# An early flag, a reordered last tile, and products that nothing reads at both ends of a gated layer kernel

## What is computed

```python
x = x + tanh(g0) * matmul(fake_quant(layernorm(x)), fake_quant(ctx))
h = layernorm(x)                               # the same row, updated
logits = h @ Wr.T                              # 4 experts, the best 2 are kept
mid    = einsum('tf,erf->ter', h, A)           # 4 experts of rank 16
delta  = sum_e softmax(kept logits)[e] * (mid[e] @ B[e].T) * SCALE
x = x + tanh(g1) * delta
```

## Time and profile before

| | before |
|---|---|
| median of 3 runs (lowest, highest) | 384.49 us (383.94, 385.21) |
| the profiled execution's own time | 386.0 us |
| its span, first to last instruction | 384.3 us |
| mean granted clock of TensorE | 0.961 of 2.4 GHz |
| busy: PE, DVE, ACT, POOL | 331.1, 290.6, 251.1, 95.9 us |
| data moved by DMA | 69.17 MB |

### The profile page before, as it was taken

How to read it: one execution, slowest core, us unless ns; L and a number is a source line. 1 busy time by engine, 2 the same in 40 slices (tenths; PEclk the granted TensorE clock), 3 DMA queues, 4 the chain that set the end, 5 groups by cost and what they waited for, 6 DMA issues and landing times. The chain is left out here.

```text
span 384.3 us, 6347 instructions
## 1 busy us (share of the span) xinstructions
PE 331.1 (86%) x2325; PEld 187.1 (49%) x2325; DVE 290.6 (76%) x715; ACT 251.1 (65%) x206; POOL 95.9 (25%) x107
## 2 busy tenths in 40 slices
PE   0148989999996689999989999999999999999374
PEld 0013434445654555555556556565556565646152
DVE  3677698679997899989756786869595969674834
ACT  1756948959999899499798065655556474743230
POOL 3100140003554341051045050504141322323000
PEclk9998999999999699999999999999999999999865
DMA  7999999950036779873641432232323201111022
GB/s 223 417 417 419 422 417 422 417 190 0 3 108 235 283 269 348 257 256 93 184 161 57 165 127 93 113 107 110 111 107 113 95 18 66 45 56 56 0 109 110
DMA packets 19185, 69.17 MB, mean 180 GB/s; under 512 B 2256, under 2 KB 2256, under 8 KB 19024
## 3 DMA queue, kind: packets, MB, share of 16 engines
q1 hardware_dynamic: 19152, 68.73, 47.9%
HBM read 51.94 MB, written 16.78 MB: 179 GB/s over the span
## 5 line engine op out<-in xcount | busy, mean ns | idle before, releaser
L658 PE MATMUL ps_main<-q,q1T 128*128 128x512 f16 x832 | 197.5, 379 | 2.1 <-ACT q1T L459 1.5
L658 PEld LDWEIGHTS ps_main<-q,q1T 128*128 128x128 f16 x832 | 77.3, 98 | 87.2 <-issue 9.0
L445 ACT ACTIVATE c_code<-q,small_tile 128x1024 uint8<-128x1024 f32 x62 | 74.7, 1239 | 24.6 <-DVE q L1118 12.7
L469 ACT ACTIVATE h_parts<-xr,small_tile 128x2048 f16<-128x2048 f32 x16 | 33.5, 2094 | 45.1 <-DVE small_tile L1196 45.1
L389 POOL TENSOR_TENSOR h_parts<-work,h_parts 128x512 f16<-128x512 f32 x30 | 34.9, 1185 | 65.9 <-ACT work L475 65.9
L1118 DVE TENSOR_SCALAR q<-c_code,small_tile 128x1024 f16<-128x1024 f16 x64 | 36.1, 566 | 15.9 <-ACT c_code L445 15.6
L1179 DVE SCALAR_TENSOR_TENSOR xr<-ps_main,small_tile,xr 128x512 f32<-128x512 f32 x52 | 38.7, 745 | 8.3 <-PE ps_main L658 8.1
L1252 DVE TENSOR_TENSOR xr<-ps_delta,xr 128x512 f32<-128x512 f32 x62 | 41.2, 681 | 4.9 <-PE ps_delta L740 3.3
L1123 DVE BATCH_NORM_STATS2 small_tile<-xr 128x6 f32<-128x512 f32 x64 | 40.9, 682 | 5.0 <-DMA xr<-in_x 5.0
L1184 DVE BATCH_NORM_STATS2 small_tile<-xr 128x6 f32<-128x512 f32 x64 | 43.6, 688 | 0.9
L481 ACT COPY hT<-ps_turn 128x1024 f16<-128x1024 f16 x32 | 31.4, 1007 | 17.9 <-PE ps_turn L692 17.8
(11 more groups left out here) (119 smaller groups left out, 393.4 us busy)
## 6 DMA issues: line engine op xcount, KB each, us to landing
q<-in_ctx SPq DMA_DIRECT2D x62, 512.0 KB, 8.7
xr<-in_x SPq DMA_DIRECT2D x32, 512.0 KB, 5.2
out_x<-xr SPq DMA_DIRECT2D x30, 512.0 KB, 2.8
h_parts<-in_B SPq DMA_DIRECT2D x1, 1024.0 KB, 16.4
q1T<-in_ctx SPq DMA_DIRECT2D x2, 512.0 KB, 8.4
out_x<-xr SPq DMA_DIRECT2D x4, 256.0 KB, 2.3
xr<-in_A SPq DMA_DIRECT2D x1, 544.0 KB, 17.0
small_tile<-in_params SPq DMA_DIRECT2D x1, 3.0 KB, 2.6
```

The costliest lines, as they stand in the source:

```text
L445: nc.scalar.activation(c_byte[:, i % 2, :], stage(i), ACT.Identity, bias=par[:, 3:4], scale=inv_s[:, 1:2]).then_inc(row_scaled, 1)
L469: nc.scalar.activation(h_hi[:, :], xr[:, b % RING, :], ACT.Identity, bias=h_bias[:, b % 2:b % 2 + 1], scale=h_rstd[:, b % 2:b % 2 + 1]).th ...
L658: mm = pe.matmul(product_bank(b, n)[:, :], q1T_of(b)[:, k, :], q2[:, batch(b), k, cols(n)], start=(k == 0), stop=(k == KT - 1))
```

## The change

Five things change.

1. `rests_of_points`, with it the flag, moves ahead of the first statistics on DVE.
2. ACT quantizes tile 0 (`scale_x(0)`) between the first and the second half row rather than behind both.
3. A new helper `keep_busy(n)` issues `n` products of 128 x 512 into `ps_main[0]` that nothing reads. It is called with 3, 7, 7 and 8 around the first two tiles' turns, and with 12 and 10 in the last tile.
4. The last tile's `h_hi` is made in two halves with a semaphore of their own, and each half of `h_lo` waits only for its half. `turn_hi` of the last tile moves ahead of the deltas 2 and 3 of tile 14. Turns, deltas and mid products are interleaved.
5. `last_delta` finishes one bank before it begins the next.

The diff, cut to its core:

```diff
@@ ACT
             scale_row(0)
+            scale_x(0)
             scale_row(1)
-            scale_x(0)
...
-            high_part(LAST)
+
+            act.wait_ge(h_bias_ready, TILES)
+            act.wait_ge(hi_turned, 2 * LAST)
+            act.wait_ge(h_lo_ready, 4 * LAST)
+            for h in range(2):
+                nc.scalar.activation(h_hi[:, half(h)], xr[:, LAST % RING, half(h)], ACT.Identity,
+                                     bias=h_bias[:, LAST % 2:LAST % 2 + 1], scale=h_rstd[:, LAST % 2:LAST % 2 + 1]).then_inc(last_hi, 1)
@@ PE
+            def keep_busy(n):
+
+                for _ in range(n):
+                    pe.matmul(ps_main[0][:, :].rearrange("p (a m) -> p a m", m=P), ident_h[:, :],
+                              ident_h[:, :].unsqueeze(1).to_broadcast([P, NB, P]), start=True, stop=True)
...
             def turn_hi(b, h):
-                pe.wait_ge(h_hi_ready, b + 1)
+                if b == LAST:
+                    pe.wait_ge(last_hi, h + 1)
+                else:
+                    pe.wait_ge(h_hi_ready, b + 1)
...
                 banks = ps_delta + ps_main
-                for n in range(2):
+                for n in range(NB):
                     pe.matmul(banks[n][:, :], gT_hi[:, :], lora_bT[:, cols(n)], start=True, stop=False)
-                pe.wait_ge(gT_ready, TILES)
-                for n in range(2):
-                    pe.matmul(banks[n][:, :], gT_lo[:, :], lora_bT[:, cols(n)], start=False, stop=True).then_inc(delta_done, 1)
-                for n in range(2, NB):
-                    pe.matmul(banks[n][:, :], gT_hi[:, :], lora_bT[:, cols(n)], start=True, stop=False)
+                    pe.wait_ge(gT_ready, TILES)
                     pe.matmul(banks[n][:, :], gT_lo[:, :], lora_bT[:, cols(n)], start=False, stop=True).then_inc(delta_done, 1)
...
                 pe.wait_ge(ident_ready, 2)
+                keep_busy(3)
                 turn_q1(0, 0)
+                keep_busy(7)
                 rows(0, 0, 0, 5, general)
+                keep_busy(7)
                 turn_q1(1, 0)
+                keep_busy(8)
                 rows(1, 0, 0, 3, general)
...
-                for n in range(NB):
-                    delta(LAST - 1, n)
+                delta(LAST - 1, 0)
+                delta(LAST - 1, 1)
+                pe.wait_ge(x1_ready, NB * LAST + 3)
+                keep_busy(12)
                 turn_hi(LAST, 0)
                 turn_hi(LAST, 1)
+                delta(LAST - 1, 2)
                 mid_hi(LAST, 0)
+                turn_lo(LAST, 0)
+                delta(LAST - 1, 3)
                 mid_hi(LAST, 1)
-                turn_lo(LAST, 0)
                 turn_lo(LAST, 1)
                 mid_lo(LAST, 0)
                 mid_lo(LAST, 1)
+                keep_busy(10)
                 turn_gate(LAST, TILES)
                 last_delta()
@@ DVE
             parameters()
+            rests_of_points()
             stats_x(0, 0)
             stats_x(0, 1)
             var_x(0)
-            rests_of_points()
             scale_of_x(0)
...
             dve.wait_ge(h_lo_ready, 4 * LAST)
+            dve.wait_ge(lo_turned, 2 * LAST)
             for h in range(2):
                 nc.vector.tensor_scalar(work[h], ...).then_inc(h2_ready, 1)
-            dve.wait_ge(h2_ready, 2 * TILES)
-            dve.wait_ge(lo_turned, 2 * LAST)
-            dve.wait_ge(h_hi_ready, TILES)
             for h in range(2):
+                dve.wait_ge(h2_ready, 2 * LAST + h + 1)
+                dve.wait_ge(last_hi, h + 1)
                 nc.vector.tensor_tensor(h_lo[:, half(h)], work[h], h_hi[:, half(h)], ALU.subtract).then_inc(h_lo_ready, 2)
```

More of the change, by code:

```diff
@@ L193, in build @@
         lo_turned, loT_ready = sem("lo_turned"), [sem("loT_ready0"), sem("loT_ready1")]
+        last_hi = sem("last_hi")
         hi_used, lo_used, mids_read, mids_scaled = sem("hi_used"), sem("lo_used"), sem("mids_read"), sem("mids_scaled")
```

## The result

| | before | after |
|---|---|---|
| median (lowest, highest), 4 runs each, taken in turn | 384.46 us (383.94, 385.21) | 375.45 us (374.84, 376.49) |
| ratio with its 95% interval | | 0.9767 [0.9739, 0.9795] |
| the profiled execution's own time, its span | 386.0, 384.3 us | 376.5, 374.7 us |
| mean granted clock | 0.961 | 0.982 |

The changed kernel is 9.0 us faster; 9.7 were forecast. The profiled execution of it was the slowest of the four, and its span of 374.7 is 0.7 to 1.6 above the others (374.0, 373.3, 373.1).

What follows compares the result with a forecast made beforehand. PE was taken as the bound in the middle, with time to be had only where PE waits at both ends. Start 3.0 plus last tile 6.8 made 9.8 us off 386.0; the median forecast was 374.8, range 372.0 to 379.0.

Steps and rivals of the forecast that it cites:

- the two terms: Start and last tile: 3.0 us from the earlier start plus 6.8 us from the last tile, together 9.8 us.
- the first term: Start: an earlier first product brings the scales of `A` 3.0 us earlier, carried to the end; bounds 0 and 3.8.
- The first product: PE at the start: code follows the earlier flag, first product at about 12.3, tile 0's turn done at 14.6 instead of 18.9.
- I take this as one delay that follows the flag: Start: the 6.56 us from flag to first transpose (flag load, branch, code behind it) move with the flag.
- DVE's code row: Around `A`: the half row's code beside POOL's first pass, 2.51 us, can't gain more than the scales do.
- From there on I find no wait with a fixed time: Middle, behind `A`: streams are relative to each other, so 3.0 us at 46 us stay 3.0 us at 350.
- The last tile: Last tile: mid products 5.8 us earlier, gate's turn 0.15 shorter, `last_delta` 0.85 less, together 6.8 us.
- The flag that gives nothing: Rival at the start: code arrives at 17.9 whatever the flag does, or low-clock products eat 1.5 us; 377.0, chance 0.17.
- the clock that falls: Rival in the last tile: clock falls, mid products gain about 2.5 us, ten products stick out by 1.7; 380.7, chance 0.11.
- The slower rival: Rival at the start: code at 17.9 and 25 exposed products cost up to 10.7 us; 388.4, chance 0.04.

Runs made afterwards that it cites:

- the flag moved back: Changed kernel with the flag's instructions put back behind tile 0's statistics on DVE, all added products kept: 377.52 us, ratio 0.9827 to the kernel before.
- the start's part alone: Kernel before plus only the early flag, ACT's swap and the 25 products around the first two turns: 381.58 us against 384.49, ratio 0.9931.
- the kernel without products: Changed kernel with all six `keep_busy` calls (47 products) left out, all orders as changed: 377.82 us, ratio 0.9826 to the kernel before.
- the end's part: Changed kernel with flag, ACT's swap and the 25 start products taken back, 12 and 10 products kept: 376.61 us, ratio 0.9796 to the kernel before.
- Repeated kernel against repeated kernel: Changed kernel run again unchanged, 375.32 us, ratio 0.9760, compared with the kernel before run again unchanged, 384.58 us. Also called the repeated pair.
- the repeated kernel before: Kernel before, run once more unchanged as a kernel of its own for its profile: 384.58 us, ratio 1.0000 to the kernel before.
- the kernel of the old order: Changed kernel with deltas 2 and 3 of tile 14 back ahead of both high turns, 12 and 10 products kept: 379.47 us, ratio 0.9869.
- the kernel with the padding: Kernel before with 22 products added only to the copy of PE's program that is not taken: 381.78 us against 385.08, ratio 0.9942.
- the kernel with the products in one copy: Changed kernel with all 47 products only in the taken copy of PE's program, execution the same: 376.24 us, ratio 0.9778 to the kernel before.

## Why the prediction was right, and where it was not

The time (375.45 against 374.8) and the two terms came out; the first term has a bound that did not hold and takes as one delay what are two.

**The first product.** Forecast 12.3, measured 12.19; tile 0's turn done at 14.6, measured 13.69 + 1.03 = 14.7; tile 1's turn ended at 24.7, forecast 24.1; DVE's copy of it at 24.74 + 2.35 = 27.1, forecast 26.5. That the code follows the flag and not the full queues is shown by the flag moved back (17.80).

**What passes on at the start.** The term of 3.0 is right in size: 2.9 us by the start's part alone (1.6 to 3.8 by the interval), a lead of 3.8 at tile 4, of which 1.9 to 3.6 arrive (below). Its bound was not. The scales of `A` were to come at most 1.74 + 0.59 + 0.65 = 3.0 earlier, and POOL's pass came 3.50 earlier, the reduction 1.87 earlier (39.64 - 37.77) and what follows it another 1.63. From its start to DVE's next step on `A` it was 4.44 us before and is 2.87 now, 1.57 less, where the two waits that I counted are 1.24; the two code rows in between now run as one piece. The cause was coarser, too. "I take this as one delay that follows the flag" was true of the 6.5 us. The 4.48 ahead of tile 0's first main products holds 2 us of another kind, the wait for the next piece of the code. That piece comes 5 to 6 us behind the first, so it follows the flag as well, and the early flag removes this wait too: 2.64 us of lead in the kernel without products. But 22 products that are never run remove it without the flag, which the prediction could not have said. For that reason the gain can't be split in one way only. By medians, the end's part with the place of its code gives 384.49 - 376.61 = 7.9, and flag, swap and the 25 products on top of that 376.61 - 375.45 = 1.2; the medians come from different jobs, so each difference is good to about 1 us. By leads at tile 4, flag and swap give 2.64 and the 25 products 1.1 on top, the place of the code alone gives 1.66 to 1.96, and all of them together 3.78. Where the products do not move the code of the taken copy, flag, swap and products give 3.07, since PE then uses up the first piece sooner and waits 3.42 us for the next.

**What was said of DVE's code row.** The prediction said that the row tied to POOL's pass can't gain more than the scales do. It holds in part. The row at 42.49 started 0.23 us ahead of POOL's pass and took 0.48; the next one, begun inside the pass, took 2.18, and another at 47.56, inside POOL's last pass over `A`, took 2.48. So the row slipped ahead, and the block fell on the next. The Trainium skill's page SBUF — State Buffer (section Terms) says that the pair of ports is locked for a full instruction and the loser blocks; the trace agrees, and shows that the row that had begun kept its time, while POOL's pass beside it took 2.60 instead of 2.49.

**The middle.** "From there on I find no wait with a fixed time" holds: the loads behind `A` are issued earlier as the program gets there earlier (tile 5's at 114.05, was 118.11). What varies is how long they take in one execution. In the profile after, the load of tile 5 was 1.5 us longer than before (5.20 against 3.72), PE then had the lower clock for 13.7 us instead of 6.9, and the lead of 3.78 at tile 4 is 1.99 at tile 5's copy (136.17 - 134.18). At the last high part it is 2.73 (360.49 - 357.75), since the shown execution of before lost 0.8 us of its own between 185 and 200 us, where PE waits for ACT behind a code row whose load lands late (1.7 us of PE's time there, 0.9 on repeat). Repeated kernel against repeated kernel, the lead is 3.57 at the end (359.68 - 356.11), with the shorter load: then 0.2 of it is lost, and in the profile after 1.9 (359.68 - 357.75 = 1.93 left of 3.78). The start's part alone lost 1.1 us in its profile between 175 and 185 us (a lead of 3.67 at 171.34, 2.60 at 182.23), with tile 5's load as short as before. So the 3.0 as a bound from `A` was too low, executions lose between 0.2 and 1.9 of the real 3.8 on the way, and that the two come to about 3.0 is in part luck.

**The last tile.** Forecast 6.8, measured 18.26 - 11.58 = 6.68 between the two profiles shown. The repeated pair gives 17.29 - 11.58 = 5.7, since the repeated kernel before had the higher clock for longer (0.66 over 360 to 370, where it was 0.57 in the earlier trace rows). Between its two profiles the last tile of before varies by 1 us with its clock, and that of the change doesn't. With the lead at the last high part the repeated pair has 3.57 + 5.71 = 9.3, its spans differ by 382.4 - 373.0 = 9.4. The steps within it came as written: halves of the high part, delta 3 directly behind the add, mid products 5.7 earlier (13.15 - 7.44; forecast 5.8), gate's turn waiting for DVE. The clock was 1.00. Of the end's gain the order, the halves and `last_delta` give 4.0 to 5.1 and the products 1.8, which the prediction did not split; of the first three only the order was tried alone (2.6 at the higher clock).

**The rivals.** The flag that gives nothing was forecast at 377.0, and the kernel with the late flag took 377.5. That is near by luck: the flag's own gain is gone there as the rival had it, and what is left of the start, a lead of 1.25, comes from the place of the code, which the rival did not have. For the clock that falls the prediction had 5.8 - 2.5 = 3.3 for the mid products and 1.7 for the exposed ten products. Measured on the kernel without products the lower clock costs 1.8 in the whole last tile: too high a price, since not all of the turns, deltas and mid products ran at the lower level (0.50 from 360 to 363, 0.96 from 363 to 366). The ten products at that level were not tried. The slower rival, 25 products exposed for up to 10.7 us, was tried by the late flag as far as it can be: 1.25 us of it showed.

**What stays open.** Why the clock stayed at 1.00 across a pause of 3.35 us in the kernel of the old order and fell after one of 3.17 in the kernel without products: the two differ in what PE did ahead of the pause (the twelve products and one more delta, or none of them), but no run separates this from the place of the pause, and three of four executions of the old order had a lower mean clock than the one profiled. And how the position within a piece sets the length of the pause: it was varied in few steps only (2.05 us before, 3.42 with the products in one copy, none with them in both). Nor is it shown why the kernel with the padding gains more in its time than its 1.66 us of lead at tile 4.

## What to carry to other kernels

Try both parts of a change alone before adding their gains: here 2.9 and 7.9 made 9.0, and the traces show that each of them happened to remove the same pause. Profile a kernel twice before reading a small difference in its middle: one load that was 1.5 us longer in one execution looked like a loss of the change. A pause with no releaser in straight code, while the DMA engines are full, is to be looked up in the queue of instruction fetches; if it falls on a fetch, moving the code (by instructions that never run, if need be) is worth trying early. At the end of a program, where engines wait for each other in turn, put what everybody waits for (turns, mid products) ahead of what waits itself (a delta that needs an add), and cheap products into the long waits if the granted clock falls there.

## What the runs showed of the hardware

- PE's code arrived 6.5 us behind the flag that picks the branch, at both times of the flag (5.71 to 12.19; 11.34 to 17.80), with the DMA engines already loading the operands.
- A piece of code can be late without any branch: 2.05 us (21.35 to 23.40; again at 23.11 in the repeated kernel) and 3.42 us in the kernel with the products in one copy, at the time when the DMA engines moved some 410 to 430 GB/s. The Trainium skill's page Runtime: NRT & Kernel Launch (section Instruction fetch mechanics) says that the cost of crossing from one block of instructions to the next is "mostly hidden"; here the measurement decides, and behind a taken branch it was not.
- The pieces of the code followed each other 5 to 6 us apart behind the branch, and where PE had stopped it went on 2.4 to 2.6 us behind a packet of the instruction queue.
- 22 products that are never executed changed the time by 2.7 to 3.3 us of 384.5, of which the pause of 2 us at the start accounts for 1.66 us (the lead at tile 4). A comparison of two kernels that differ in their number of instructions carries such a term in it.
